# Two output adds moved ahead of the state read, and twenty empty places removed from a vector engine's fill order

## The reference

```python
xn = layernorm(x)
q, k, v = (short_conv(xn @ W, conv) for W, conv in ...)   # 4 taps, then silu
def step(S, inp):                       # scanned over the tokens
    S = S * jnp.exp(g_t)[..., None, None]
    u = (v_t - jnp.einsum('bhk,bhkv->bhv', k_t, S)) * b_t[..., None]
    S = S + jnp.einsum('bhk,bhv->bhkv', k_t, u)
    o_t = jnp.einsum('bhk,bhkv->bhv', q_t, S)
    return (S, o_t)
o = rms_norm(o) * norm_w * silu(xn @ Wg)
out = x + o @ Wo + experts(xn)
```

## Time and profile before

| | |
|---|---|
| median of 3 runs | 2642.53 us (2633.9 to 2644.04) |
| the profiled execution | 2633.9 us, its span 2632.2 us |
| PE busy | 2266.7 us (86%), 36541 matmuls |
| DVE busy | 1903.0 us (72%), 3913 instructions |
| ACT busy | 1354.1 us (51%) |
| POOL busy | 1137.5 us (43%) |

### The profile page before, as it was taken

How to read it: one execution, slowest core, us unless ns; L and a number is a source line. 1 busy time by engine, 2 the same in 40 slices (tenths; PEclk the granted TensorE clock), 3 DMA queues, 4 the chain that set the end, 5 groups by cost and what they waited for, 6 DMA issues and landing times. The chain is left out here.

```text
span 2632.2 us, 93819 instructions
## 1 busy us (share of the span) xinstructions
PE 2266.7 (86%) x36541; PEld 1651.1 (63%) x36542; DVE 1903.0 (72%) x3913; ACT 1354.1 (51%) x3667; POOL 1137.5 (43%) x1143
## 2 busy tenths in 40 slices
PE   4652999999987889899888989989898888989987
PEld 4541999999963646556565655746556565655646
DVE  5664232323228888988889899888988989888894
ACT  0001444344326655656656566655656656566663
POOL 3774444444433426253342624436253342624333
PEclk9997999999988999999999999999999999999998
DMA  5574222222210010100101000010100101000010
GB/s 168 193 248 152 72 72 73 71 72 72 72 55 21 17 44 11 36 22 25 32 15 44 21 27 23 25 44 5 42 22 25 33 14 44 23 24 22 25 29 16
DMA packets 105644, 135.05 MB, mean 51 GB/s; under 512 B 39360, under 2 KB 78816, under 8 KB 105056
## 3 DMA queue, kind: packets, MB, share of 16 engines
q0 software_dynamic: 23552, 61.38, 7.5%
q1 hardware_dynamic: 62448, 40.55, 5.8%
q10 hardware_dynamic: 19312, 28.33, 3.0%
HBM read 76.18 MB, written 54.00 MB: 49 GB/s over the span
## 5 line engine op out<-in xcount | busy, mean ns | idle before, releaser
L1458 DVE SCALAR_TENSOR_TENSOR att_cv<-att_psA,att_cw,att_cv 128x508 f32<-128x508 f32 (+2 forms) x660 | 479.2, 737 | 7.6
L1789 POOL TENSOR_TENSOR att_Sd<-att_S,att_mst 128x1024 f32<-128x1024 f32 x128 | 242.9, 1903 | 505.1 <-DVE att_S L1572 482.0
L999 PE MATMUL att_psA<-att_xt,att_wqkv 128*128 128x512 f32 x880 | 425.3, 616 | 17.0 <-DMA att_xt<-xn_cols 12.6
L1122 PE MATMUL att_psS<-att_W,att_ktok 128*128 128x128 f32 x2048 | 258.8, 280 | 12.1 <-DVE att_S L1572 6.4
L999 PEld LDWEIGHTS att_psA<-att_xt,att_wqkv 128*128 128x128 f32 x880 | 156.7, 193 | 178.7 <-issue 159.5
L734 PE MATMUL moe_psHT<-moe_xT,moe_w1s 128*128 128x128 f32 x2176 | 267.5, 276 | 0.0
L1122 PEld LDWEIGHTS att_psS<-att_W,att_ktok 128*128 128x128 f32 x2048 | 242.5, 193 | 32.9 <-issue 17.2
L675 ACT ACTIVATE moe_hT<-moe_psHT,moe_b1T 128x128 f32<-128x128 f32 x544 | 155.1, 368 | 201.1 <-PE moe_psHT L734 201.1
L744 PE MATMUL moe_psY<-moe_w,moe_hT 128*128 x1088 | 257.2, 379 | 0.0
L734 PEld LDWEIGHTS moe_psHT<-moe_xT,moe_w1s 128*128 128x128 f32 x2176 | 256.1, 193 | 0.2
L701 DVE TENSOR_TENSOR moe_y<-moe_psY,moe_b2b 128x256 f32<-128x256 f32 x136 | 57.8, 425 | 271.1 <-PE moe_psY L744 271.1
(11 more groups left out here) (247 smaller groups left out, 4382.1 us busy)
## 6 DMA issues: line engine op xcount, KB each, us to landing
expert_out<-moe_y POOLq DMA_DIRECT2D x136, 128.0 KB, 2.0
route_x_in<-in_L_attn_x_dram SPq DMA_DIRECT2D x64, 128.0 KB
xn_rows<-route_xn ACTq DMA_DIRECT2D x16, 512.0 KB, 3.6
xn_cols<-route_xnT ACTq DMA_DIRECT2D x16, 512.0 KB, 3.8
moe_w<-in_L_ffn_W_dram ACTq DMA_DIRECT2D x2, 4096.0 KB, 24.5
att_xt<-xn_cols SPq DMA_DIRECT2D x16, 512.0 KB, 4.4
att_xr<-in_L_attn_x_dram SPq DMA_DIRECT2D x64, 128.0 KB, 2.7
out_dram<-att_xr SPq DMA_DIRECT2D x256, 32.0 KB, 1.7
```

Of the source, the lines that this page charges most:

```text
L999: last = MM(pair_bank(m, j)[:, h, :], wqkv[:, c, (2 * j + h) * P:(2 * j + h + 1) * P], xt[:, c, :], start=(c == 0), stop=(c == DC - 1))
L1122: last = MM(pS[:, h // 4, 2 * DV * (h % 4):2 * DV * (h % 4) + 2 * DV], ktok[:, c % 2, h, :], W[:, h, 2 * two:2 * two + 2, :], start=True, ...
L1458: last = V.scalar_tensor_tensor(out=late, in0=by_lane(pair_bank(m, j)[:, h, :])[:, :, 0:LT - d], scalar=cw[:, 2 * j + h, TAPS - 1 - d:TAPS ...
L1789: G.tensor_tensor(new, old, bc(mst[:, par, c, 4 + 2 * two:6 + 2 * two, :], 3, DV), op=ALU.mult).then_inc(s["sd_done" if two else "sd_half" ...
```

## The change

In `others()` inside VectorE's `after_keys`, the adds of outputs 0 and 1 are issued right after the last tap, ahead of `read` and `residual`, and the 20 empty places are removed with their constant. The other engines' programs are not edited.

```diff
         NCONST = 10
-        ALONE = 20
...
                     yield from taps(f, par, 8)
                     yield from taps(f, par, 9)
-                    for _ in range(ALONE):
+                    if m is not None:
+                        out(m, 0)
+                        yield
+                        out(m, 1)
                         yield
                     read(f, par, 0)
                     yield
                     residual(f, 0)
                     yield
-                    if m is not None:
-                        out(m, 0)
-                        yield
-                        out(m, 1)
-                        yield
```

## The result

The changed kernel takes 2715.45 us (median of 4 runs, 2714.05 to 2717.91), the kernel before 2639.23 in the same comparison: a ratio of 1.029, with a 95% interval of 1.0265 to 1.0316. It is slower by 76.2 us (the interval is 70 to 83); 76.5 were forecast. The profiled execution took 2710.17 us with a span of 2708.4, against 2632.2 before; the spans differ by 76.2 too. Every engine executes as many instructions as before, and VectorE is busy 1903.3 us against 1903.0. The added time is idle time, apart from some 24 us in which TensorE's matmuls lasted longer (2290.3 us against 2266.7).

A forecast was written before the change was run, and what follows sets the result against it. VectorE and TensorE, both full, bound the kernel through their hand-overs, arriving at the solve within 0.2 us. 63.0 + 2 - 11.5 - 1 + 24 = 76.5 us on the 2642.53 median gave 2719 us, range 2687 to 2746.

The forecast's parts named there:

- The stall: VectorE's output 0 add after the last tap waits for TensorE's products; inverse later by 4.2 us in 15 groups, 63.0 us.
- The collision with GpSimd: An elimination step on VectorE lengthened beside a GpSimd instruction, 1.10 us against 0.40; 0.7 us saved if it no longer hits.
- TensorE's lateness: At the solve, TensorE already comes after the inverse, so VectorE can be later by this for nothing: minus 11.5 us.
- Stores and row loads: SP issues them about 4 us earlier; VectorE's wait for row loads, 3.3 us, should vanish: minus 1 us.
- The clock: TensorE's hole before the solve brings the lower clock level: 2.0 us in 12 groups, 24 us.
- The first group: It has no outputs; read and residual only move ahead and wait for their product: 2 us.
- The stall alone: Rival: the clock stays where it was and only the wait is paid, 52.5 us, 2695 us; chance 0.24.
- Low through the update: Rival: the low clock lasts through the state update, 12 groups by 4.26 us, 103.6 us in all, 2746 us; chance 0.13.
- Absorbed: Rival: VectorE catches up in the scan after the solve; less than 13 us left, some 2650 us; chance 0.05.
- Faster: Rival: transfers moved ahead no longer hold TensorE up, giving back up to 14.8 us, 2628 us; chance 0.02.

The follow-up runs named there:

- fifteen_empty: Changed kernel with 15 empty places ahead of the adds of outputs 0 and 1, read and residual: 2643.15 us, ratio 1.0007 to the kernel before.
- seven_empty: Changed kernel with 7 empty places ahead of the adds of outputs 0 and 1, read and residual: 2662.22 us, ratio 1.0089 to the kernel before.
- read_first: Changed kernel with read and residual right after the last tap and the two output adds behind them: 2731.56 us, ratio 1.0334 to the kernel before.
- hole_filled: Changed kernel with TensorE doing the next second-head key projection two extra times right before the solve, result overwritten: 2708.53 us, ratio 1.0238 to the kernel before.
- second_head_first: Changed kernel with the real projection of the next group's second head moved from behind the solve to right before it: 2708.99 us, ratio 1.0264.
- before_warm_two: Kernel before plus two extra TensorE matmuls, one ahead of the queries, one between queries and read of the state: 2644.98 us, ratio 1.0012.

## Why the prediction was right

*The stall.* Forecast 4.2 us in 15 groups, 63.0 us, from the place of the last tap and the end of the products. The inverse comes 4.30 us later, 64.6 us; the wait in front of the adds is 4.24 or 4.25 us in every one of the 15 groups. fifteen_empty and seven_empty confirm the way of counting: 4.3 us of elimination ahead takes the stall away, 2.2 us leaves 2.2. read_first shows that the length is set by the distance to TensorE's product and not by what kind of instruction waits.

*The collision with GpSimd.* I left open whether its 0.7 us stay. For the most part they stay: one elimination step takes 0.92 to 1.27 us beside GpSimd's instruction in 11 of 15 groups, as in 11 of 15 before (1.10 to 1.27). In two groups, the one shown among them, only 0.3 of the 0.7 us are left, and they fall on the residual (L1563), which takes 1.02 us where it takes 0.69 elsewhere, beside this instruction (L1776 of before):

```profile
1561.97 1.04 POOL L1773 TENSOR_TENSOR att_qg<-tri_q,att_mst 128x512 f32<-128x512 f32 x1 [25.56 <-DMA att_mst<-token_stats]
```

By the Trainium skill, page "SBUF — State Buffer", section "SBUF: two separate sides", a VectorE instruction with two SBUF inputs and a GpSimd instruction that reads SBUF exclude each other on a shared port pair. The trace agrees: the lengthened instructions, elimination steps and residuals, have two SBUF inputs. The read (L1556) takes one input from PSUM. It ran beside the same GpSimd instruction for 0.53 us in the group shown, and kept its 0.69 us.

*TensorE's lateness.* Forecast minus 11.5 us. The inverse is later by 64.6 us in all and the solve by 53.0: 11.6 were absorbed. In the changed kernel the solve follows the inverse after 0.15 us in all 15 groups.

*Stores and row loads.* Forecast minus 1 of 3.3 us. The wait is gone, but the way from state add to next last tap is the same within 0.02 us per group, so it was worth nothing measurable. SP issues the stores at 1560.83, 4.7 us after the last tap, where it was 8.6.

*The clock.* Forecast 2.0 us in 12 groups, 24 us. Measured 19.9 us, which is 2.2 us in each of 9 newly slow groups, and 1.7 in the first group. So the price was about right and the number of groups too high: the hole stayed above 2.5 us in 11 groups, not 12, one of them kept full clock, and the last group was slow already, which the forecast did not take off. hole_filled shows the cause. The rule of the Trainium skill that was weighed in the prediction (page "TensorE: Matmul & The Clock Gate", section "Why this matters for your kernels": an idle gap sends the clock down) agrees with ten of the eleven holes of 2.79 us and more, and not with the one of 3.56 us.

*The first group.* Forecast 2 us, measured 4.3: the inverse comes 2.6 us later (the read waits 2.05), and 1.7 are the clock, which I had not counted there. The terms that were off cancel: the clock was forecast 4.1 us too high, the first group 2.3 and the stall 1.6 too low. The closeness of 76.2 to 76.5 is luck by about 4 us, and it is closer than the measurement can tell (70 to 83 us).

*The rivals.* "The stall alone" would have been 52.5 us; it is refuted by the 20 us that hole_filled takes off between solve and state add. "Low through the update" (4.26 us per group) is refuted by the update's own time: 1.95 us in 11 of the 15 groups of the changed kernel, 2.2 in three, and 3.79 only in the last, as before the change. "Absorbed" is refuted by 90.06 against 90.09 us from state add to next last tap. "Faster" is refuted by the stall, and fifteen_empty shows that even without the stall the earlier transfers give nothing back that can be measured.

## What to carry to other kernels

Empty places in a hand-written order are no waste where they hold an instruction back until its input is there: an in-order engine that reaches a wait too early pays with everything queued behind it. Count the distance from the place of the instruction to the end of its producer on the other engine, and put that much independent work in between; here ten elimination steps of 0.43 us were just enough. Where two engines arrive at a hand-over together, a delay of one goes through in full; where the other is late anyway, that part is free (11.6 of 64.6 us here). A long hole on TensorE can cost once more through its clock.

## What the runs showed of the hardware

In the changed kernel, holes of 2.79 to 5.89 us on TensorE, after a thin stretch, were followed by the clock at 1.2 GHz in 10 of 11 groups, and the solve took up to 1.97 us instead of 1.09. With holes of 0 to 2.90 us (seven_empty) the state add was late by more than 0.4 us in one group besides the last. The length of the hole alone does not decide it: in second_head_first a hole of 1.37 to 2.13 us ahead of the solve, with nothing between solve and update, was followed by a slow update in six groups. Extra matmuls do not simply buy full clock: in before_warm_two none of the low stretches fell between solve and state add, and the clock was low for longer later in the group. A VectorE instruction with two SBUF inputs went from 0.40 to 1.10 us beside a GpSimd instruction of 1.07 us; the read, with one input from PSUM, kept its 0.69 us beside one of 1.04 us.
